# The first part of the last layer's head in a four-layer graph network kernel: split gather-back, later bias adds, and a norm moved from VectorE to ScalarE

## What is computed

```
x = x + _L2_ffn_ref(_layernorm(x), ...)          # each node: a gated sum of the rows of K=6 experts
x = x + _L3_gnn_ref(_layernorm(x), src, dst, deg, W1, b1, W2, b2)
    # xn = layernorm(x)
    # agg = segment_sum(xn[src], dst) / deg
    # out = xn @ W1.T + b1 + agg @ W2.T + b2
x = x + _L3_ffn_ref(_layernorm(x), ...)          # 8 experts, top 2
```

## Time and profile before

| | us |
|---|---|
| median of 3 runs | 2436.04 |
| lowest and highest | 2435.09, 2436.72 |
| the profiled execution's own time | 2432.22 |
| its span (first to last instruction) | 2430.5 |
| granted clock of TensorE, mean | 0.965 |

### The profile page before, as it was taken

The page is one execution under the profiler, slowest core; times in us unless marked ns, Lnnn a source line. Parts: engine busy times, 40 slices in busy tenths (PEclk is TensorE's granted clock), DMA queues, the critical chain, the costliest instruction groups (busy, mean ns, idle before and its releaser), DMA issues. The chain is left out here.

```text
span 2430.5 us, 39014 instructions
## 1 busy us (share of the span) xinstructions
PE 2278.4 (94%) x14326; PEld 1510.7 (62%) x14326; DVE 1113.9 (46%) x2631; ACT 703.1 (29%) x1366; POOL 614.5 (25%) x624
## 2 busy tenths in 40 slices
PE   5798969999999999999999999999999997989998
PEld 4475537766766765647657567566665665567775
DVE  8732895545545556545425325326262333530102
ACT  0423343322333332315315315325211211112111
POOL 0463666505524530010100100101113442111110
PEclk9898989999999999999999999999989998989999
DMA  3122017516525542011011011010026766458885
GB/s 92 43 69 85 1 55 226 150 35 219 149 60 177 168 128 103 13 47 53 23 45 53 24 45 53 23 54 34 22 114 222 253 210 204 116 220 318 311 293 197
DMA packets 68400, 285.96 MB, mean 118 GB/s; under 512 B 18650, under 2 KB 18778, under 8 KB 60286
## 3 DMA queue, kind: packets, MB, share of 16 engines
q1 hardware_dynamic: 35771, 192.15, 22.8%
q0 software_dynamic: 32448, 91.31, 12.4%
HBM read 407.54 MB, written 26.23 MB: 178 GB/s over the span
## 5 line engine op out<-in xcount | busy, mean ns | idle before, releaser
L86 PE MATMUL ps<-XT,W 128*128 128x250 f32 (+1 forms) x1200 | 334.8, 435 | 3.5 <-ACT XT L1420 1.6
L86 PEld LDWEIGHTS ps<-XT,W 128*128 128x128 f32 x1200 | 228.9, 193 | 106.5 <-issue 22.2
L1150 PE MATMUL ps<-XN,W 128*128 128x512 f32 x498 | 258.9, 603 | 2.6 <-ACT GT L1472 2.6
L1856 POOL TENSOR_TENSOR H<-H,RB 125x512 f32<-125x512 f32 x40 | 50.5, 1267 | 724.3 <-DVE XN L2179 611.7
L86 PE MATMUL ps<-W,HT 128*128 128x512 f32 (+1 forms) x312 | 141.5, 608 | 0.8 <-ACT HT L3242 0.5
L86 PEld LDWEIGHTS ps<-HT,W 128*128 128x128 f32 x1088 | 126.9, 195 | 8.7 <-issue 7.7
L86 PE MATMUL ps<-HT,W 128*128 128x128 f32 x1088 | 127.1, 279 | 0.8 <-DVE HT L3253 0.8
L2572 POOL DMA_INDIRECT result_rows<-KT,LOGC x61 | 62.1, 1018 | 251.2 <-DVE KT L3273 197.2
L1126 POOL DMA_INDIRECT XT<-node_rows,LOGC x81 | 77.2, 953 | 174.4 <-DMA node_rows<-V 122.3
L1288 PEld LDWEIGHTS ps<-P,QT 128*128 128x128 f32 x672 | 89.9, 195 | 45.0 <-issue 45.0
L1288 PEld LDWEIGHTS ps<-P,KT 128*128 128x128 f32 x672 | 88.1, 192 | 39.7 <-issue 39.7
(11 more groups left out here) (666 smaller groups left out, 4593.6 us busy)
## 6 DMA issues: line engine op xcount, KB each, us to landing
W<-in_L_ffn_Wgud SPq DMA_DIRECT2D x92, 960.0 KB
W<-in_L_ffn_w SPq DMA_DIRECT2D x36, 2048.0 KB, 8.4
W<-in_L_gnn_Wqkv SPq DMA_DIRECT2D x4, 3072.0 KB, 9.9
H<-in_L_ffn_Wgud SPq DMA_DIRECT2D x11, 960.0 KB
XN<-in_L_ffn_Wgud SPq DMA_DIRECT2D x11, 960.0 KB
V<-in_L_ffn_Wgud SPq DMA_DIRECT2D x11, 960.0 KB
P<-in_L_ffn_Wgud SPq DMA_DIRECT2D x11, 960.0 KB
RB<-in_L_ffn_Wgud SPq DMA_DIRECT2D x11, 960.0 KB
```

The source lines that it names most:

```text
L86: last = nc.tensor.matmul(out, lhs(k), rhs(k), start=(k == 0), stop=(k == nk - 1))
L1150: nc.tensor.matmul(b.ps[:, n % PR, :], b.EAT[:, t * 128:(t + 1) * 128], We[layer], start=True, stop=True)\
L1856: ins = nc.gpsimd.tensor_tensor(b.H[0:R, t, :], b.H[0:R, t, :], b.RB[0:R, at:at + D], ALU.add)
```

## The change

Three edits in the head:

1. The gather-back of tile 0 is split into three transfers of two places each, with a semaphore each; VectorE's sums of tile 0 start when the first has landed. The other tiles keep their one transfer.
2. GpSimd's five bias adds wait until VectorE has made all five first adds (`first_read` at T) instead of following each norm. What waited for the bias add at the first add now waits for it at the add of the second product; the first add waits for `xn_ready` instead, so that the norm has read X.
3. The first norms move to ScalarE: VectorE computes only 1/std and -mean/std (two instructions of one element per partition, `affine`), and ScalarE computes XN = X/std - mean/std as an activation, between its square root and its copy of the transposed columns. The second norms stay on VectorE.

```
@@ SyncE
-                for lo, hi in PARTS:
-                    sp.dma_start(rows[t][lo:hi], back[t * R + lo:t * R + hi, :, :]).then_inc(tile_in[t], 16)
+                for first, last, done in pieces(t):
+                    for lo, hi in PARTS:
+                        sp.dma_start(rows[t][lo:hi, first:last], back[t * R + lo:t * R + hi, first:last, :]).then_inc(done, 16)
...
+    def pieces(t):
+        if t:
+            return [(0, K2, tile_in[t])]
+        return [(0, 2, tile_in[0]), (2, 4, s["in5"]), (4, K2, s["in6"])]
@@ GpSimd
+            pool.wait_ge(s["first_read"], T)
             for t in range(T):
-                pool.wait_ge(s["xn_ready"], t + 1)
                 nc.gpsimd.tensor_tensor(b.X[0:R, t, :], b.X[0:R, t, :], b.RB[0:R, 0:D], ALU.add).then_inc(s["biased"], 1)
@@ ScalarE
             for t in range(T):
                 root("var", "std", t)
+                act.wait_ge(s["affine"], t + 1)
+                nc.scalar.activation(b.XN[0:R, t, :], b.X[0:R, t, :], ACT.Identity, scale=b.rstd[0:R, t:t + 1],
+                                     bias=b.var[0:R, t:t + 1]).then_inc(s["xn_ready"], 1)
                 columns_out("t_mm", "xt_ready", t)
@@ VectorE
+            def affine(t):
+                dve.wait_ge(s["var"], t + 1)
+                dve.wait_ge(s["std"], t + 1)
+                c.link(v.reciprocal(b.rstd[0:R, t:t + 1], b.std[0:R, t:t + 1]))
+                v.scalar_tensor_tensor(b.var[0:R, t:t + 1], b.mv[0:R, t, 0:1], -1.0, b.rstd[0:R, t:t + 1], ALU.mult,
+                                       ALU.mult).then_inc(s["affine"], 1)
...
             def first_added(t):
-                dve.wait_ge(s["biased"], t + 1)
+                dve.wait_ge(s["xn_ready"], t + 1)
                 dve.wait_ge(s["first_mm"], t + 1)
...
-                normed(t, "var", "std", "xn_ready")
+                affine(t)
...
             for t in range(T):
                 dve.wait_ge(s["second_mm"], t + 1)
-                dve.wait_ge(s["first_read"], t + 1)
+                dve.wait_ge(s["biased"], t + 1)
```

More of the change, by code:

```diff
@@ L2803, in l3_block @@
     TE = T * NE
-    s = semaphores(p, "g3", "chain", "in0", "in1", "in2", "in3", "in4", "summed", "var", "std", "xn_ready", "t_mm", "xt_ready",
+    s = semaphores(p, "g3", "chain", "in0", "in1", "in2", "in3", "in4", "in5", "in6", "affine", "summed", "var", "std", "xn_ready", "t_mm", "xt_ready",
                    "deg_mm", "deg_read", "row_summed", "biased", "agg_mm", "agg_ready", "first_mm", "first_read", "second_mm",
@@ L3042, in normed @@
                                 ALU.subtract, ALU.mult).then_inc(s[ready], 1)
-            def gathered_back(t):
[L3045 to L3050, removed]
+            def affine(t):
[4 more added lines that the diff above has]
+                                       ALU.mult).then_inc(s["affine"], 1)
+            def gathered_back(t):
+                for first, last, done in pieces(t):
+                    dve.wait_ge(done, 32)
+                    for k in range(first, last):
+                        if k:
+                            dve.wait_ge(s["summed"], K2 * t + k)
+                        v.scalar_tensor_tensor(b.X[0:R, t, :], rows[t][:, k, :], r2.gates[:, k * T + t:k * T + t + 1],
+                                               b.X[0:R, t, :], ALU.mult, ALU.add).then_inc(s["summed"], 1)
                 dve.wait_ge(s["summed"], K2 * (t + 1))
             def first_added(t):
-                dve.wait_ge(s["biased"], t + 1)
+                dve.wait_ge(s["xn_ready"], t + 1)
                 dve.wait_ge(s["first_mm"], t + 1)
```

## The result

| | median, us | lowest to highest | runs |
|---|---|---|---|
| before | 2436.31 | 2435.07 to 2437.88 | 10 |
| changed | 2441.72 | 2438.78 to 2444.77 | 10 |

The changed kernel takes 1.0023 times as long as before, 95% interval [1.0015, 1.0031]: 5.4 us more, where the forecast was 4.5 more and 0.2% is 4.9. The time lies in the predicted range. Its middle is beyond the bound of 0.2%, but the interval reaches from 3.7 to 7.6 us and holds that bound, so "slower by over 0.2%" and "the same" are not told apart.

What follows compares the result with a forecast made beforehand. TensorE is busy 94% of the span and waits in the head, where it and VectorE are level at 7.71 us per tile. Path -0.3 plus clock 4.8 gives +4.5 us, 2440.5; range 2435.0 to 2442.4.

Steps and rivals of the forecast that it cites:

- Levels: Head, middle tiles: TensorE and VectorE arrive within hundredths of a microsecond, period 7.71 us, so relieving one gains nothing.
- the sum: Head path: 2.1 us won at tile 0, 1.8 lost over four norms, 0.3 us sooner; with 4.8 for clock, +4.5.
- The split: Tile 0's gather-back: VectorE never waits, sums end 2.57 us sooner, first turn at 2063.00 with the later norm included.
- its other end: Tile 0's gather: pieces land together at 2058 or tile 1 later, nothing gained; 2438.1 with clock up, chance 0.03.
- The norm on ScalarE: Head's five first norms: reciprocal to turn takes 1.25 us against 0.79, so 0.46 us more on the path each.
- The held adds: GpSimd's five bias adds, 1.27 us each, are covered behind the fifth first add; they free 0.89 us in four sums.
- The clock: TensorE's gaps between tiles grow from 1.51 to 1.97 us; three clock falls at 1.6 us each cost 4.8 us.
- its slower rival: Head loop: more low-clock time than three falls, over 10.6 us in all; 2441.1 to 2443.5 us, chance 0.18.
- The chances: Whole kernel against the 0.2% bound: faster 0.03, the same 0.72, slower 0.25.
- The forecast's own range: Whole kernel with two or three clock falls, 2439.0 to 2440.8, widened for measurement to 2438.2 to 2441.6 us.
- The likeliest case: Two or three clock falls in the head's gaps between tiles: 2439.0 to 2440.8 us, chance 0.50.
- The rival in which the clock holds: Head loop: TensorE's clock stays up across the longer gaps, everything else as forecast; 2435.7 us, chance 0.26.

Runs made afterwards that it cites:

- split only: Kernel before with only tile 0's gather-back split into three transfers: 2433.86 us, ratio 0.9991.
- norm only: Kernel before with only the five first norms moved to ScalarE: 2442.34 us, ratio 1.0029.
- the longer gap: Kernel before with one more VectorE pass into XN ahead of each first norm, overwritten by it: 2442.72 us, ratio 1.0029.
- the filled kernel: Changed kernel with two added matmuls of 500 columns before the transposes of tiles 1 to 4: 2433.55 us, ratio 0.9988; repeated on another chip 2434.45 us, 0.9995.
- the last experiment: Changed kernel with VectorE's norm part before the previous tile's first add, plus five matmuls of 500 columns before tile 0's transposes: 2432.07 us, ratio 0.9987.

## Why the prediction was right, point by point

**Levels.** Right. VectorE and TensorE arrive together in the loop; the held adds alone freed 0.9 us per tile and 0.82 came back as a wait. In the changed kernel the same relief shows as part of the waits in front of the first adds. Their size was put too low: about 1 us, where they are 1.66 us at full clock. The rows of before give that number: the new period of 8.16 us less what VectorE then needs, 7.71 - 0.89 - 0.55 + 0.2 = 6.47. The waits are not on the path, so the sum does not suffer.

**The split.** Right: the sums start 0.11 us behind the degree rows with no wait, and the first turn stands at 2066.03, which less the 3.03 us of the later start is 2063.00, the predicted number. The whole time confirms the size only roughly (split only: 2.3 us for 2.1, interval 0 to 4.4). The price of its other end does not follow from the sum: without the split the 2.1 us of the path are missing, which gives 2437.8 with the clock up, not 2438.1.

**The norm on ScalarE.** Right: 0.39 us from reciprocal to activation, then 0.81 us, and 1.86 us from first add to turn (2074.90 to 2076.76). The gap is 1.97 us.

**The held adds.** Right as to their cover, GpSimd in the changed kernel:

```profile
2113.44 6.17 POOL L2893 TENSOR_TENSOR X<-X,RB 125x512 f32<-125x512 f32 x5 [61.06 <-DVE X L3074]
```

All five are over by 2119.6, at 1.23 us each for the predicted 1.27. With no GpSimd add beside them, no sum takes 1.65 us. The Trainium skill ("SBUF — State Buffer", section "Who interferes with whom") says that a VectorE instruction with two SBUF inputs contends with a GpSimd one that reads SBUF, and the trace agrees. But the 3.6 us that would come back by that rule alone did not: the held adds by themselves changed nothing (1.0003).

**The clock.** The mechanism was right: gaps of 1.97 us bring falls, the price of one was put at 1.6 us and is 1.69. That there were three was an estimate ("about three in four") for which no row stood; that it came out exactly is in part luck. One term was left out of the sum: the clock in tile 0 was taken to rise as before; it rose 5.3 us after the turn and not 3.1, so tile 0 took 8.87 us instead of 7.78, 1.1 us more. The prediction named this in its slower rival. With it, -0.3 + 1.1 + 3 x 1.69 = 5.9 us, and the pair of traces has 5.86. But the 1.1 us cannot be put down to the change: norm only and the longer gap, both without the split, show 8.69 and 9.18 us for the same tile, and the trace of before has the shortest of all. Without it the sum is 4.8 us, which the interval of the measured 5.4 holds as well.

**The chances.** The bound between "the same" and "slower" lies at 4.9 us and the time at 5.4, with 0.25 on that side. The forecast's own range reached to 2441.6; the median is 2441.7, or 2441.4 when the 5.4 us are put on the 2436.04 that the forecast started from. Three falls at its own price make 2440.5, so the 2440.8 that it gives as their upper end is 0.3 us too high. The likeliest case was what happened. The rival in which the clock holds is what the filled kernel shows, level with before in its repeat.

**What stays open.** Which gaps are followed by a fall. In this loop gaps of 1.51 to 1.79 us never were. Those of 1.90 to 1.97 us were in three of four cases in each of four traces: behind turns 1, 3 and 4 in the changed kernel, its repeat and norm only, behind turns 2, 3 and 4 with the longer gap. But in the last experiment neither the gap of 1.98 us in front of turn 0 nor that of 2.13 us in front of turn 3 was. And behind the loop, in the routing of the changed kernel, where shorter matmuls stand around it, one of only 1.76 us was (the gap, then the work behind it):

```profile
2144.47:2146.23 1.76, 0.00 (x0) 0.00 (x1) 1.21 (x4) 0.29 (x1) 0.00 (x0) 1.00 0.00 0
2146.45:2149.75 3.30, 3.30 (x18) 3.30 (x17) 0.00 (x0) 1.87 (x2) 0.00 (x0) 0.50 0.26 78
```

Length alone does not decide, and no border between 1.79 and 1.90 us is shown. Nor is it settled when the clock rises in tile 0: in the changed kernel 5.3 us after the turn, in its repeat 4.8, before 3.1, in split only 5.9.

## What to carry to other kernels

Before work is moved off a busy engine onto an idle one, look at which engine waits for the result and how long its idle gap becomes: 0.46 us more on each of five hand-offs was worth 2 us by itself and 5 more through TensorE's clock. When two engines arrive together in a loop, relieving one of them buys a wait; the order of the instructions on that engine (the norm ahead of the add of the tile before) made the changed kernel 10 us faster by ratios. Where the clock had not fallen it was worth about 2 us by the trace, as much as the split, and not clear of noise in the whole time. If a gap cannot be made shorter, a matmul of no use in it can be worth more than the time that it takes. The split shows one thing more: when a transfer leaves the path, ask what stands behind it, here TensorE's count of the degrees at half clock.

## What was not expected of the hardware

Behind the gaps of 1.90 to 1.97 us the clock falls not in the gap but 0.2 to 1.4 us after TensorE has taken up work again (0.2 in the repeat of the changed kernel, whose turn 3 is at 2090.10), and it stays at 1.2 GHz for 3.4 us although TensorE is busy without a break (3.40 of 3.40 us in the window above). Longer gaps are another case: in that of 4.41 us it fell 1.8 us before work began again. And filler matmuls ahead of the very first turn only moved the low stretch: in the 4.41 us idle that followed, the clock was lost again. The Trainium skill ("TensorE: Matmul & The Clock Gate", section "Why this matters for your kernels") warns of longer gaps than those that cost the clock here, 1.90 to 1.97 us; the measurement decides.
